# Half-precision copies and remainders of the hidden layer, two chunks at a time and in another order

## The reference, cut to what matters

```
def step(acc, params):
    W1a_e, b1a_e, W1b_e, b1b_e, W2_e, b2_e, w_e = params
    a = xf @ W1a_e + b1a_e
    b = xf @ W1b_e + b1b_e
    y = jax.nn.silu(a) * b @ W2_e + b2_e
    return (acc + w_e[:, None] * y, None)
```

## Time and profile before

| | |
|---|---|
| median of three runs | 609.79 us (608.49 to 610.49) |
| profiled execution | 609.25 us, of which the span from first to last instruction is 607.4 us |
| busy share of the span | PE 79%, PEld (weight loads) 63%, DVE 76%, ACT 70%, POOL 56% |
| expert stage | first transposes at 391.63 us, last matmul of the last `project_out` at 572.62 us |

### The profile page before, as it was taken

One profiled execution on the slowest core, in us unless ns is written; L12 is line 12 of the kernel. 1 busy time (PEld: TensorE's weight loads), 2 busy tenths in 40 slices (PEclk: granted clock), 3 DMA queues, 4 the chain that ended last, 5 costly groups with the idle time before them and its releaser, 6 DMA issues.

```text
span 607.4 us, 19940 instructions
## 1 busy us (share of the span) xinstructions
PE 479.3 (79%) x5529; PEld 380.5 (63%) x5530; DVE 461.9 (76%) x1571; ACT 422.7 (70%) x1108; POOL 343.0 (56%) x501
## 2 busy tenths in 40 slices
PE   4579997889888988888899751199999999999500
PEld 1356775667666766666677530198888888888400
DVE  5576889889888988898988455277877777778456
ACT  3458876878787878777886632088888888898500
POOL 5443455767676767677765466214555545545553
PEclk9989999999999999999999875599999999999755
DMA  8321122211221232112211030512212211111076
GB/s 236 83 72 36 42 55 59 63 47 57 75 64 41 54 78 61 39 56 78 60 41 43 31 94 27 121 42 57 66 51 56 61 48 53 55 53 46 19 229 186
DMA packets 53668, 41.53 MB, mean 68 GB/s; under 512 B 7554, under 2 KB 48341, under 8 KB 53616
## 3 DMA queue, kind: packets, MB, share of 16 engines
q1 hardware_dynamic: 43056, 29.12, 18.2%
q0 software_dynamic: 4544, 8.54, 4.4%
q10 hardware_dynamic: 6016, 3.24, 1.9%
HBM read 24.80 MB, written 12.78 MB: 62 GB/s over the span
## 4 chain that ended last, share of the span: by engine, by line
PE 53%; DVE 23%; issue 9%; DMA 5%; ACT 5%; POOL 3%; DVEq 1%; SPq 1%; ACTq 0%; POOLq 0%
DVE nmax L797 5%; PE bank L1319 5%; PE bank L1127 5%; PE bank L1162 5%; PE bank L1320 4%; PE bank L1321 4%; PE bank L1340 3%; PE bank L1341 3%; PE bank L1342 2%; PE bank L1140 2%; PE bank L1151 2%; PE bank L1139 2%; PE bank L1165 2%; PE bank L1177 2%; PE bank L1115 2%
## 5 line engine op out<-in xcount | busy, mean ns | idle before, releaser
L797 DVE TENSOR_REDUCE nmax<-bank 128x3 f32<-128x384 f32 x256 | 139.0, 550 | 26.2 <-PE bank L1127 24.3
L1127 PE MATMUL bank<-cb,c 128*128 128x256 bf16 x512 | 141.5, 276 | 0.0
L602 ACT ACTIVATE probs<-bank 128x384 f32<-128x384 f32 x256 | 124.0, 496 | 21.1 <-PE bank L1127 19.5
L555 POOL DMA_INDIRECT expert_outs<-probs,number_of x78 | 78.8, 1011 | 92.5 <-ACT probs L705 79.3
L1037 DVE SCALAR_TENSOR_TENSOR probs<-bank,b_sb,probs 128x256 f32<-128x256 f32 x156 | 71.7, 480 | 52.2 <-ACT probs L716 52.0
L1319 PE MATMUL bank<-xt,we_hi 128*128 128x256 f16 x312 | 86.0, 276 | 2.1 <-issue 0.8
L1320 PE MATMUL bank<-xt,we_hi 128*128 128x256 f16 x312 | 85.8, 275 | 0.0
L1321 PE MATMUL bank<-xt,we_lo 128*128 128x256 f16 x312 | 85.8, 275 | 0.0
L696 ACT ACTIVATE hh<-probs 128x256 f16<-128x256 f32 x156 | 64.1, 411 | 18.9 <-DVE probs L1037 16.4
L469 POOL DMA_INDIRECT expert_rows<-send,pos_i x64 | 63.5, 992 | 24.2 <-issue 12.4
L1151 PE MATMUL bank<-q_max,k_pad 128*128 128x256 f16 x256 | 70.8, 277 | 1.1 <-ACT probs L602 1.0
(11 more groups left out here) (179 smaller groups left out, 1326.9 us busy)
## 6 DMA issues: line engine op xcount, KB each, us to landing
g_in<-expert_rows SPq DMA_DIRECT2D x39, 132.0 KB
k_pad<-qk_t SPq DMA_DIRECT2D x128, 32.0 KB, 1.9
mod_b<-mod_rows SPq DMA_DIRECT2D x16, 256.0 KB, 3.2
we_lo<-expert_outs SPq DMA_DIRECT2D x16, 256.0 KB, 3.6
wstage<-in_L_ffn_W1a_dram SPq DMA_DIRECT2D x16, 128.0 KB, 2.4
wstage<-in_L_ffn_W1b_dram SPq DMA_DIRECT2D x16, 128.0 KB, 2.5
wstage<-in_L_ffn_W_dram SPq DMA_DIRECT2D x16, 128.0 KB, 2.7
out_dram<-we_lo ACTq DMA_DIRECT2D x16, 128.0 KB, 3.2
```

The costliest lines, as they stand in the source:

```text
L555: pool.indirect_dma_start(out=outs, out_offset=bass.IndirectOffsetOnAxis(ap=number_of[:, r, s:s + 1], axis=0), in_=y_sb[:, r, s, :], in_of ...
L602: nc.scalar.activation(probs[:, k % (2 * HG)], col_bank[k % 2][:, 0:S + P], ACT.Exp, scale=SM_SCALE).then_inc(probs_ready, 1)
L797: nc.vector.tensor_reduce(nmax[:, k], row_bank[k % 2][:, 0:3 * P].rearrange("p (c t) -> p c t", t=P), AX.X, ALU.max, negate=True).then_inc ...
L1127: return mm(diagonal, ident16, mask.unsqueeze(1).broadcast_to([P, 2, P]), start=False, stop=True, skip_group_check=True)
```

## The change

The copies are made for two chunks at a time (`high(j, half)`, 512 elements per partition), and so are the remainders (`low(j, half)`). The first pair of tile j is copied behind silu 2, ahead of `weigh`; the second pair is copied in the next tile, behind its silu 0, and its remainder is taken behind the next tile's h 0. The first pair's remainder stands last in VectorE's tile. `act_hh` and `vec_hl` count two per tile and no longer four.

```
-            def high(j, f):
-                act.wait_ge(vec_h, times(j, FB, f + 1))
+            def high(j, half):
+                two = slice(2 * half, 2 * half + 2)
+                act.wait_ge(vec_h, times(j, FB, 2 * half + 2))
                 if due(times(plus(j, -2), 1, 1)):
                     act.wait_ge(pe_y, times(plus(j, -2), 1, 1))
-                nc.scalar.activation(hh[:, j[1] % 2, f], h32[:, f], ACT.Copy).then_inc(act_hh, 1)
+                nc.scalar.activation(hh[:, j[1] % 2, two], h32[:, two], ACT.Copy).then_inc(act_hh, 1)
...
                     if f == 1 and more:
                         save_x(plus(j, 1))
-                    if f == 2 and finished:
-                        weigh(plus(j, -2))
+                    if f == 0 and following:
+                        high(plus(j, -1), 1)
                     if f == 2:
+                        high(j, 0)
+                        if finished:
+                            weigh(plus(j, -2))
                         read_next_experts(j)
-                    if f:
-                        high(j, f - 1)
-                high(j, FB - 1)
...
-            def low(j, f):
-                vec.wait_ge(act_hh, times(j, FB, f + 1))
-                nc.vector.tensor_tensor(hl[:, j[1] % 2, f], h32[:, f], hh[:, j[1] % 2, f], ALU.subtract).then_inc(vec_hl, 1)
+            def low(j, half):
+                two = slice(2 * half, 2 * half + 2)
+                vec.wait_ge(act_hh, times(j, 2, half + 1))
+                nc.vector.tensor_tensor(hl[:, j[1] % 2, two], h32[:, two], hh[:, j[1] % 2, two], ALU.subtract).then_inc(vec_hl, 1)
...
-                    if due(times(plus(j, -1), FB, f + 1)):
-                        vec.wait_ge(vec_hl, times(plus(j, -1), FB, f + 1))
+                    if due(times(plus(j, -1), 2, f // 2 + 1)):
+                        vec.wait_ge(vec_hl, times(plus(j, -1), 2, f // 2 + 1))
...
-                    if f >= 2:
-                        low(j, f - 2)
+                    if f == 0 and following:
+                        low(plus(j, -1), 1)
                     if f == 2:
                         read_next_experts(j)
-                low(j, FB - 2)
-                low(j, FB - 1)
+                low(j, 0)
...
-                pe.wait_ge(vec_hl, times(j, FB, FB))
+                pe.wait_ge(vec_hl, times(j, 2, 2))
```

More of the change, by code:

```diff
@@ L707, in _, with tile @@
             known_experts, read_next_experts = experts_of(act)
-            def tile(j, more=True, finished=True):
+            def tile(j, more=True, finished=True, following=True):
                 e = known_experts(j)[0]
@@ L718, in tile @@
                         save_x(plus(j, 1))
-                    if f == 2 and finished:
-                        weigh(plus(j, -2))
+                    if f == 0 and following:
+                        high(plus(j, -1), 1)
                     if f == 2:
+                        high(j, 0)
+                        if finished:
+                            weigh(plus(j, -2))
                         read_next_experts(j)
-                    if f:
-                        high(j, f - 1)
-                high(j, FB - 1)
             save_x(tile_number(0))
-            tile(tile_number(0), finished=False)
+            tile(tile_number(0), finished=False, following=False)
             tile(tile_number(1), finished=False)
@@ L731, in _ @@
             tile(tile_number(NT - 1), more=False)
+            high(tile_number(NT - 1), 1)
             weigh(tile_number(NT - 2))
@@ L1020, in _, with tile @@
             vec.wait_ge(table, TABLE_STEPS)
-            def low(j, f):
-                vec.wait_ge(act_hh, times(j, FB, f + 1))
-                nc.vector.tensor_tensor(hl[:, j[1] % 2, f], h32[:, f], hh[:, j[1] % 2, f], ALU.subtract).then_inc(vec_hl, 1)
+            def low(j, half):
+                two = slice(2 * half, 2 * half + 2)
+                vec.wait_ge(act_hh, times(j, 2, half + 1))
+                nc.vector.tensor_tensor(hl[:, j[1] % 2, two], h32[:, two], hh[:, j[1] % 2, two], ALU.subtract).then_inc(vec_hl, 1)
             known_experts, read_next_experts = experts_of(vec)
-            def tile(j, finished=True):
+            def tile(j, finished=True, following=True):
                 e, last, before_last = known_experts(j)
@@ L1058, in _ @@
             e, last = tile(tile_number(NT - 1))
+            low(tile_number(NT - 1), 1)
             bias_out(tile_number(NT - 2), last)
```

## The result

Eleven runs of each kernel gave a median of 613.1 us for the changed one (610.59 to 615.45) and 608.73 us for the one before (606.49 to 610.49). The ratio is 1.0079, with a 95% interval of 1.006 to 1.0098: slower by 4.4 us as the medians differ and by 4.8 as the ratio has it, where 614.3 us were forecast. The profiled execution has a span of 611.1 us against 607.4.

The account below looks back on a forecast made before the run. A loop of ScalarE and VectorE was taken as the bound, not TensorE. 36 steps × 0.15 = 5.4, plus 0.47, less 0.8, gave 5.1 on 609.25: 614.3 us; range 610.2 to 618 for 8 in 10.

Parts of the forecast that it names:

- What bounds the kernel: Expert stage before the change: ScalarE and VectorE limit the 4.42 us tile; TensorE follows with about 0.24 us to spare.
- The loop: Closed round of ScalarE and VectorE in each steady tile after the change: 4.57 us against 4.42, 0.15 longer.
- the nine steps: Start-to-start: h 0, second low pair, h 1, first `hh` pair, `weigh`, silu 3, h 3, first low pair, `bias_out`, next h 0.
- What is hidden: TensorE's way round, second low pair through `project_out` to the next second low pair: 4.27 us, fitting under 4.57.
- the cover: The 4.57 us ScalarE and VectorE round hiding TensorE's 4.27 with 0.3 to spare; without it TensorE sets the pace.
- The prices of the pairs: Durations of the 512-element instructions: 0.63 us for an `hh` copy pair on ScalarE, 0.68 for a low pair on VectorE.
- Loop ends: Every eighth tile costs 0.76 us extra; 0.2 taken off at each of four ends, 0.8 us less in all.
- The last tile: From silu 3 to `project_out` at the stage's end: 2.70 us where it was 2.23, costing 0.47 once.
- Sum: Whole kernel: 36 tile steps × 0.15 = 5.4, plus 0.47 for the last tile, less 0.8: 5.1 us slower.
- The rival "the work saved counts": Expert stage: less ScalarE work shrinks the tile to 4.18 and TensorE sets the end, 8.9 us faster, 600.4 us; chance 0.07.

Follow-up runs that it names:

- the pairs alone: Against the changed kernel, copies and remainders stay in pairs but stand in the order of the kernel before: 601.93 us, ratio 0.9889 to the kernel before.
- `bias_out` late: Against the changed kernel, VectorE's `bias_out` moved behind h 2, from between the first low pair and h 0: 625.91 us, ratio 1.027 to the kernel before.
- `project_out` in halves: Against the changed kernel, `project_out` waits for the first low pair at its start and the second half way through: 613.47 us, ratio 1.0066 to the kernel before.

## Why the prediction was right

*What bounds the kernel* was right: not TensorE. For the kernel before, the pairs alone show it: they change nothing of TensorE's work and brought the tile from 4.42 to 4.33. For the changed kernel, splitting TensorE's wait moved nothing, and moving or shortening pieces of work on ScalarE and VectorE moved the tile between 4.18 and 5.09.

*The loop.* Eight of the nine steps were within 0.01 us of the forecast (0.39, 0.60, 0.51, 0.54, 0.58, 0.60, 0.40, 0.60, 0.33 against 0.41, 0.59, 0.52, 0.54, 0.59, 0.59, 0.41, 0.59, 0.33), and the first within 0.02; the tile came to 4.55 where 4.57 was worked out. Taking the first low pair or `weigh` out of it, or halving the low pairs, freed the tile to 4.18 to 4.23.

*What is hidden.* TensorE's loop was worked out at 4.27 and set the tile at 4.23 once the cover was gone. The part from silu 0 to the low pair was put too long, at 0.36 + 0.63 + 0.14 = 1.13 by way of the copy; with `weigh` behind silu 3 it took 1.03 (silu 0 at 469.79, h 0 at 470.42, the low pair at 470.82, 0.04 after the copy's end).

*The prices of the pairs*, 0.63 and 0.68, were measured as 0.626 and 0.682.

*Loop ends.* Eight tiles of the changed kernel, by its `save_x` at the same places as the earlier trace rows:

```profile
449.36 0.60 ACT L690 ACTIVATE xt<-bank 128x512 f16<-128x512 f16 x1
...
486.21 0.59 ACT L690 ACTIVATE xt<-bank 128x512 f16<-128x512 f16 x1
```

36.85 us, 0.45 over 8 × 4.55, against 0.76 before. I had taken 0.2 off; it was 0.3 here. In the eight tiles ahead of these nothing came off: 37.18 us against 36.05, 0.78 and 0.69 over eight steady tiles. The choice went the right way by luck, without a reason that the runs have confirmed.

*The last tile.* `project_out` started 573.64 − 571.03 = 2.61 us after silu 3 where 2.23 had been: 0.38 and not 0.47. Its first and last matmul, in the kernel before and in the changed one:

```profile
570.45 0.23 PE L1340 MATMUL bank<-we_hi,hh 128*128 x1 [2.81 <-DVE hl L1024]
...
572.62 0.31 PE L1342 MATMUL bank<-we_hi,hl 128*128 x1
```

```profile
573.64 0.23 PE L1343 MATMUL bank<-we_hi,hh 128*128 x1 [2.45 <-DVE hl L1027]
...
574.98 0.22 PE L1345 MATMUL bank<-we_hi,hl 128*128 x1
```

That is 2.17 us against 1.34. In the profile before, the granted clock was 1.00 until 570.84 and 0.50 from there to 573.00 (1.2 GHz in place of 2.4), after TensorE had waited 2.81 us; in the changed kernel's profile it stayed at 1.00 after a wait of 2.45. The forecast has no term for this.

*Sum.* 36 × 0.13 = 4.7, and 0.38, less 4 × 0.31: 3.8 us by these terms; the profiled spans differ by 3.7, the runs by 4.8 ± 1.2. That 3.8 and 3.7 agree so closely is luck. The four turns of the hardware loop are 3.42 us longer in all, so their ends gave back 4 × 8 × 0.13 − 3.42 = 0.7 and not 4 × 0.31; the 0.8 of the forecast was near this. The terms then make 4.3. The stage itself, from its first transposes to the first matmul of the last product, took 573.64 − 390.11 = 183.53 us against 570.45 − 391.63 = 178.82: 4.7 longer. The spans differ by less because in these two profiles the stage began 1.5 us earlier in the changed kernel, though nothing ahead of it was edited, and its last product took 0.83 less; 1.3 us more came behind it. So the forecast of 5.1 was a little high in the tile step and the last tile.

*The rival "the work saved counts".* The work was saved, but off the loop that sets the pace. The advice of the Trainium skill, page "VectorE: DVE Perf Modes", section "Rules for kernel authors", to minimize the count of operations, holds here where the order leaves the loop alone: the pairs in the order of before made the kernel 1.1% faster. No run pairs the remainders and not the copies, so how much of this is VectorE's isn't shown; the sum on record for that run puts it on ScalarE's copies. The rule doesn't hold by itself: the same pairs with one remainder put between h 0 and h 1 and another between h 3 and the next h 0 made it 0.8% slower.

## What to carry to other kernels

When engines hand work to each other in turn, write down each way round of the tile as start-to-start steps, and let the longest closed one set the forecast; busy shares and idle gaps do not show which it is. On the longest way round, an instruction put in front of one that another engine waits for counts with its whole start-to-start step (0.60 us for a low pair here); the same instruction behind it, in a wait, left the loop, and the tile became shorter by 0.32 us, down to the next way round. Before moving a step out of the longest loop, add up the next longest, which takes over.

## What was not expected of the hardware

- An instruction that must wait for the one just ahead of it on the same engine started 0.21 to 0.23 us after that one's end (h behind a low pair, with the second low pair behind h 1 and with `bias_out` late), while VectorE's instructions without such a wait started 0.08 us before the end of the one ahead (0.60 from a low pair of 0.68 to h 1).
- The cost of a hardware loop's end differed between the orders that were run, by the second turn of each: 0.2 us per eight tiles with the pairs in the order of before, 0.45 with the change, 0.76 before, 1.14 with the first low pair behind h 2, whose eight tiles are these:

```profile
447.76 0.59 ACT L690 ACTIVATE xt<-bank 128x512 f16<-128x512 f16 x1
...
482.74 0.60 ACT L690 ACTIVATE xt<-bank 128x512 f16<-128x512 f16 x1
```

  It looks as if the orders with copies reaching over into the next tile pay more, but the kernel before, which has none, paid 0.76, and the changed kernel with `project_out` in halves has such an order too and paid 0.3 (36.68 us for eight tiles from 455.29). No run isolates the cause. It stays open.
